# A first close whose output projection is made in three fp32r products of high and low parts

## The reference

```python
Q, K, V = (circulant(layernorm(x), c, b) for c, b in (wq, wk, wv))   # 16 heads of 16
weights = softmax(einsum('bqhd,bkhd->bhqk', Q, K) * scale)
out_merge = einsum('bhqk,bkhd->bqhd', weights, V).reshape(bs, seq_len, dm)
out = circulant(out_merge, wo_c, wo_b)        # the output projection
x = x + out                                   # x1
x = x + moe(layernorm(x))                     # its router needs layernorm(x1) @ gate_W.T
```

## Time and profile before

| | before |
|---|---|
| median of 3 runs | 2192.7 us (2192.51 to 2196.58) |
| the profiled execution's own time | 2198.27 us |
| its span, first to last instruction | 2196.5 us |
| mean granted TensorE clock | 0.947 |
| PE busy over the span | 1971.4 us (90%) |
| ACT busy | 1384.5 us (63%) |
| DVE busy | 1200.6 us (55%) |
| POOL busy | 757.1 us (34%) |
| exponentials of the first attention, L1236 and L1248 | 256 and 256 |
| output projection, L798 | 240 records |

### The profile page before, as it was taken

The page is one execution under the profiler, slowest core; times in us unless marked ns, Lnnn a source line. Parts: engine busy times, 40 slices in busy tenths (PEclk is TensorE's granted clock), DMA queues, the critical chain, the costliest instruction groups (busy, mean ns, idle before and its releaser), DMA issues. The chain is left out here.

```text
span 2196.5 us, 37925 instructions
## 1 busy us (share of the span) xinstructions
PE 1971.4 (90%) x12275; PEld 1136.5 (52%) x12275; DVE 1200.6 (55%) x2196; ACT 1384.5 (63%) x1581; POOL 757.1 (34%) x643
## 2 busy tenths in 40 slices
PE   6999999999946699999999999958789989998797
PEld 5722333333332588888888888846422222222255
DVE  4520242434357624333333333356599999999867
ACT  5589999999933233233233323236589999999833
POOL 2000000100010242344244244111178888888722
PEclk9999999999965699999999999979899999999998
DMA  6744433543110520221221222049725345263021
GB/s 202 229 95 68 81 77 47 116 58 82 35 40 8 232 83 25 90 80 34 86 80 38 82 87 80 23 184 336 213 46 121 58 90 103 42 142 58 2 87 67
DMA packets 76839, 203.64 MB, mean 93 GB/s; under 512 B 13028, under 2 KB 28134, under 8 KB 74536
## 3 DMA queue, kind: packets, MB, share of 16 engines
q1 hardware_dynamic: 66920, 179.22, 30.7%
q0 software_dynamic: 6816, 18.62, 2.5%
q10 hardware_dynamic: 2896, 3.16, 0.6%
HBM read 338.84 MB, written 60.03 MB: 182 GB/s over the span
## 5 line engine op out<-in xcount | busy, mean ns | idle before, releaser
L1202 PE MATMUL psum<-A_qa,A_ka 50*128 50x512 f32 x2048 | 416.4, 472 | 50.3 <-DVE A1f_probs L1280 22.8
L1202 PEld LDWEIGHTS psum<-A_qa,A_ka 50*128 50x128 f32 x2048 | 178.5, 187 | 503.1 <-DVE A1f_probs L1280 266.3
L2350 PE MATMUL psum<-e_w_high,e_xT 128*128 x1136 | 386.9, 402 | 3.9 <-DVE e_xT L2300 3.8
L1386 POOL TENSOR_TENSOR A1f_probs<-A1f_probs,A1f_bias 128x512 f32<-128x512 f32 x256 | 330.2, 1300 | 116.3 <-ACT A1f_probs L1248 116.2
L1236 ACT ACTIVATE A0f_probs<-psum 128x1024 f32<-128x1024 f32 x256 | 307.6, 1201 | 22.7 <-PE psum L1202 21.5
L1280 DVE SCALAR_TENSOR_TENSOR A1f_probs<-psum,A1f_bias 128x1024 f32<-128x1024 f32 x256 | 311.0, 1215 | 15.8 <-PE psum L1202 13.0
L2307 DVE TENSOR_TENSOR e_hT<-psum,e_hT 128x1024 fp32r<-128x1024 f32 x71 | 87.0, 1225 | 422.4 <-ACT e_hT L2271 422.4
L1248 ACT ACTIVATE A0f_probs<-psum 128x1024 f32<-128x1024 f32 x256 | 308.9, 1207 | 0.4 <-PE psum L1202 0.4
L1240 ACT ACTIVATE A1f_probs<-A1f_probs 128x1024 f32<-128x1024 f32 x256 | 272.8, 1065 | 30.3 <-DVE A1f_probs L1280 29.7
L1218 PE MATMUL psum<-A1f_probs,v 128*32 128x512 f32 x2048 | 276.4, 611 | 15.6 <-POOL A1f_probs L1386 13.8
L1218 PE MATMUL psum<-A0f_probs,v 128*32 128x512 f32 x2048 | 274.3, 608 | 0.0
(11 more groups left out here) (280 smaller groups left out, 2708.2 us busy)
## 6 DMA issues: line engine op xcount, KB each, us to landing
e_w_raw<-in_experts SPq DMA_DIRECT2D x73, 3072.0 KB, 10.8
qk_parts<-L_part SPq DMA_DIRECT2D x64, 512.0 KB, 3.7
A_qa<-qk_parts SPq DMA_DIRECT2D x192, 128.0 KB, 4.2
A_ka<-qk_parts SPq DMA_DIRECT2D x192, 128.0 KB, 6.3
om<-results SPq DMA_DIRECT2D x16, 512.0 KB, 8.5
A1f_bias<-tables SPq DMA_DIRECT2D x16, 384.0 KB, 8.5
A1f_bias<-tables SPq DMA_DIRECT2D x16, 320.0 KB, 10.0
L_x<-in_x SPq DMA_DIRECT2D x8, 512.0 KB, 7.5
```

The costliest lines, as they stand in the source:

```text
L1202: mm = e.matmul(ps[:, side * HALF:(side + 1) * HALF], self.qk.ka[rows, s, pair, kt * P:(kt + 1) * P].bitcast(FP32R), self.qk.qa[rows, s, p ...
L1386: e.tensor_tensor(fourth, fourth, self.bias_of(*w[1:], slice(self.FOURTH, GH)).rearrange("p h q -> p (h q)"), ALU.mult).then_inc(self.mult ...
L2350: mm = e.matmul(out, left[part].bitcast(FP32R), moving.bitcast(FP32R), start=start and i == 0, stop=stop and i == 2)
```

## The change

`heavy(u)` now yields 4 tiles of 256 columns for every unit. A tile is six matmuls on fp32r operands: for each of two 128-row chunks, high part of om with high part of wo, high with low, and low with high. POOL makes the parts by two instructions each, a copy that rounds to fp32r and a subtraction, in new jobs `part` that stand right behind the turn of each odd g (16 jobs on 128 x 512 elements), and once for wo at the start. PE's first tile of a unit waits for `parted` in the place of `turned`. Tiles are put into the list in steps kt = 1 and kt = 6 of a half, and in steps kt = 5, 6 and 7 (two in kt = 7) of the very last half. DVE's add is one of 128 x 256 in the place of two of 128 x 128.

```diff
-    def pieces(self, u):
-
-        return ((0, D),) if u == self.LAST else ((0, D // 2), (D // 2, D))
+        self.om_high, self.om_low = (sb(f"c_om_{name}", [P, 2, DC, HALF]) for name in ("high", "low"))
+
+
+
+    def parts(self, b):
+
+        return [("part", 2 * b + half, c) for c in range(DC) for half in range(2)]
 
     def heavy(self, u):
         for t in range(self.T):
-            for a, z in self.pieces(u):
-                yield [("wo", u, t, a, z)] + ([("stats", u, t)] if z == D else [])
+            yield [("wo", u, t), ("stats", u, t)]
...
+        self.part(e, self.wo_high[:, :, :], self.wo_low[:, :, :], self.wo[:, :, :])
+
+    def part(self, e, high, low, whole):
+        steps = self.m.pool
+        a = steps.of(e.tensor_copy(high.bitcast(FP32R), whole))
+        e.wait_ge(steps.sem, a)
+        e.tensor_tensor(low.bitcast(FP32R), whole, high, ALU.subtract).then_inc(self.parted, 1)
 
     def pool(self, e, job):
         kind, u = job[0], job[1]
         s, steps = u % 2, self.m.pool
+        if kind == "part":
+            c, b, half = job[2], u // 2, u % 2
+            e.wait_ge(self.turned, 4 * b + half + 2 * c + 1)
+            if u >= 2:
+                e.wait_ge(self.wo_full, self.wo_count(u - 2, self.T - 1))
+            self.part(e, self.om_high[:, s, c, :], self.om_low[:, s, c, :],
+                      self.omT[:, b, c, half * HALF:(half + 1) * HALF])
         if kind == "fetch":
             e.wait_ge(self.x_in[s], DMA * (u // 2 + 1))
             e.tensor_tensor(self.x[:, s, :, :], self.x[:, s, :, :], repeat(self.bo[:, :], self.T),
...
-            t, a, z = job[2:]
-            b, half = u // 2, u % 2
-            if t == 0 and a == 0:
-                if u == 0:
-                    self.wait_weights(e)
-                e.wait_ge(self.turned, 4 * b + half + 3)
-            at = (half * self.T + t) * P
-            for k in range(DC):
-                mm = e.matmul(ps[:, 0:z - a], self.omT[:, b, k, at:at + P], self.wo[:, k, a:z], start=(k == 0),
-                              stop=(k == DC - 1))
+            t = job[2]
+            if t == 0:
+                e.wait_ge(self.parted, 1 + 4 * (u // 2) + u % 2 + 3)
+            tile = slice(t * P, (t + 1) * P)
+            products = [(om, w, k) for k in range(DC)
+                        for om, w in ((self.om_high, self.wo_high), (self.om_high, self.wo_low), (self.om_low, self.wo_high))]
+            for i, (om, w, k) in enumerate(products):
+                mm = e.matmul(ps[:, 0:D], om[:, u % 2, k, tile].bitcast(FP32R), w[:, k, :].bitcast(FP32R),
+                              start=(i == 0), stop=(i == len(products) - 1))
             mm.then_inc(self.wo_full, 1)
         elif kind == "xn":
             t = job[2]
...
-            e.wait_ge(self.wo_full, self.wo_count(u, t, z))
-            e.tensor_tensor(self.x1[:, s, t, a:z], self.m.wide(slots.slot(job))[:, 0:z - a], self.x[:, s, t, a:z],
+            e.wait_ge(self.wo_full, self.wo_count(u, t))
+            e.tensor_tensor(self.x1[:, s, t, :], self.m.wide(slots.slot(job))[:, 0:D], self.x[:, s, t, :],
                             ALU.add).then_inc(self.wo_out, 1)
...
-                if self.order[at][0] == NG - 1:
-                    u = 2 * self.order[at][1] + half
+                g, b = self.order[at]
+                u = 2 * b + half
+                if g % 2:
+                    work.append(("part", u, g // 2))
+                if g == NG - 1:
                     heavy.extend(close.heavy(u))
                     waiting.append(u)
 
         def begin():
             work.extend(heavy.pop(0))
-            if waiting and len(heavy) % len(list(close.heavy(0))) == 0:
+            if waiting and len(heavy) % close.T == 0:
                 u = waiting.pop(0)
                 light.extend(chain(close.behind(u), close.logits(u)))
 
@@ -1004,9 +1022,9 @@
                     if len(behind) >= self.lag:
                         products()
                     ends = at == last and half == 1
-                    if heavy and (kt in (3, 5, 7) or ends):
+                    if heavy and (kt >= 5 if ends else kt in (1, 6)):
                         begin()
-                        if ends and heavy and kt >= BT - 2:
+                        if ends and heavy and kt == BT - 1:
                             begin()
                     if light:
                         work.extend(light.pop(0))
@@ -1581,8 +1599,9 @@
```

More of the change, by code:

```diff
@@ L674, in __init__ @@
         self.turned, self.wo_full, self.wo_out = sem("c_turned"), sem("c_wo_full"), sem("c_wo_out")
+        self.parted = sem("c_parted")
         self.measured, self.rooted, self.normed = sem("c_measured"), sem("c_rooted"), sem("c_normed")
@@ L684, in allocate @@
         self.wo, self.bo = sb("wo", [P, DC, D]), sb("bo", [P, D])
+        self.wo_high, self.wo_low = sb("wo_high", [P, DC, D]), sb("wo_low", [P, DC, D])
         self.gate, self.gate_rows = sb("gate", [P, DC, EXPERTS]), sb("gate_rows", [P, EXPERTS, D])
@@ L722, in logits, with wo_count @@
             yield [("scale", u)]
-    def wo_count(self, u, t, z):
-        return 2 * self.T * u + (t + 1 if u == self.LAST else 2 * t + (2 if z == D else 1))
+    def wo_count(self, u, t):
+        return self.T * u + t + 1
     def load_weights(self, e):
@@ L748, in sync @@
             if u >= 2:
-                e.wait_ge(self.wo_out, self.wo_count(u - 2, self.T - 1, D))
+                e.wait_ge(self.wo_out, self.wo_count(u - 2, self.T - 1))
             e.dma_start(self.x[:, s, :, :], self.x_src[u, :, :, :]).then_inc(self.x_in[s], DMA)
         elif kind == "store_x1":
-            e.wait_ge(self.wo_out, self.wo_count(u, self.T - 1, D))
+            e.wait_ge(self.wo_out, self.wo_count(u, self.T - 1))
             if u:
@@ L831, in dve @@
             t = job[2]
-            e.wait_ge(self.wo_out, self.wo_count(u, t, D))
+            e.wait_ge(self.wo_out, self.wo_count(u, t))
             n = steps.of(e.bn_stats(self.stats[:, t, :], self.x1[:, s, t, :]))
@@ L1583, in __init__ @@
         self.close = close
-        parts = chain([[("fetch", 0), ("fetch", 1)]], *(chain(close.heavy(u), close.behind(u), close.logits(u))
-                                                        for u in range(close.UNITS)))
+        parts = chain([[("fetch", 0), ("fetch", 1)]],
+                      *(chain([close.parts(u // 2)] if u % 2 == 0 else [], close.heavy(u), close.behind(u),
+                              close.logits(u)) for u in range(close.UNITS)))
         self.jobs = [j for part in parts for j in part]
```

## The result

| | before | after |
|---|---|---|
| median of 7 runs each | 2194.42 us (2192.51 to 2201.33) | 2205.66 us (2199.34 to 2208.83) |
| the profiled execution's own time | 2198.27 us | 2205.16 us |
| its span | 2196.5 us | 2203.1 us |
| mean granted TensorE clock | 0.947 | 0.944 |

The change makes the kernel slower: the ratio is 1.0048, with an interval of 1.0036 to 1.0060, so +10.5 us (+7.9 to +13.2). The profiled executions show +6.9 of it.

The account below looks back on a forecast made before the run. ACT's exponentials were taken to set the pace. Three times eight halves +8.8, the last half -5.0 and the tail +1.5 gave +5.3 us on the median of 2192.7, so 2198.0 us, range 2191 to 2205.

Parts of the forecast that it names:

- main case: The whole kernel gets slower, to 2198.0 us, with its own range of 2194.5 to 2201.5; chance 0.45.
- B: Rival: PE's clock stays low for long behind each stall, a stalled tile costs 8.0 us; +11.3, 2204.0 us; chance 0.15.
- C: Rival: matmul work isn't shortened, 0.96 us per tile, 0.49 lost by each of 21; +9.3, 2202.0 us; chance 0.07.
- three times eight halves: From the turn of u = 0 to that of u = 6: each eight halves cost 8.5 us instead of 5.6, +8.8 in all.
- the last half: Tiles of u = 6 move to kt = 5, 6, 7, 7; the stall and its low clock go: -5.0 us.
- the tail: Behind the turn of u = 7, PE starts 2.1 us later because parts come between: +1.5 us.
- stalled first tile: At u = 0, 2, 4 PE waits for turn and part: 4.7 us at full clock, 1.5 for the clock, 6.2 each.
- ordinary tile: Each of 21 tiles in the eight halves outside the stalls costs 0.33 us, bounds 0 and 0.49.
- ring: A tile shifts the ring of three, so scores wait for an exponential one place later: 0.28 to 0.35 us lost.
- 12 other parts: POOL's part jobs outside the stalls and the tail run beside work that does not wait: no cost.
- A: Rival: PE's clock is back within 1 us, a stalled tile costs 5.2 us; +1.2, 2193.9 us; chance 0.25.
- D: Rival: the spacing decides, the 21 ordinary tiles cost nothing and the clock holds; -8.0, 2184.7 us; chance 0.08.

Follow-up runs that it names:

- kept_busy: The changed kernel with 14 small matmuls on constants ahead of PE's wait for the first tile of u = 0, 2 and 4; 2201.81 us, ratio 1.0043.
- late_4_7: The changed kernel with its tiles in steps kt = 4 and 7 in the place of 1 and 6; 2184.68 us, ratio 0.9962.
- even_steps: The changed kernel with tiles in steps kt = 0 and 4, the last part job in two and POOL's bias add in four; 2182.54 us, ratio 0.995.
- parts_beside: The kernel before with the 16 part jobs added on POOL, their results read by nobody; 2193.2 us, ratio 0.9992.
- bias_in_four: The changed kernel with POOL's bias add made in four instructions of 128 x 256; 2207.89 us in a single execution.
- split_last: The changed kernel with the last part job (u = 7) made in two, 128 and 384 columns; 2205.96 us in a single execution.
- plain_1_6: The changed kernel's tiles and steps, but each tile in two fp32 matmuls straight from omT, without parts on POOL; 2196.12 us, ratio 1.001.
- late_3_6: The changed kernel with its tiles in steps kt = 3 and 6 in the place of 1 and 6; 2180.91 us in a single execution.

## Why the prediction was right on the sign and short on the size

On the base that the prediction used, 2192.7 us, the ratio gives 2203.2: slower, as forecast, but by 10.5 us and not 5.3. That lies inside the stated 2191 to 2205 and outside the main case's own 2194.5 to 2201.5: the mechanism was right, but the range held only because it had been widened for rivals B and C. The sum by its own steps, against the stage of the profiled execution:

| term | predicted | measured |
|---|---|---|
| three times eight halves | +8.8 | +12.4 |
| the last half | -5.0 | -4.6 |
| the tail | +1.5 | +1.3 to the last statistics, +0.7 to the sinkhorn |
| sum | +5.3 | +8.5 in the stage |

*The stalled first tile* was right in place and nearly so in size. PE idle was to be some 4.5 us, released by POOL's subtraction: 4.44. ACT idle some 5 us: 5.63. The clock near 0.5: 0.50. The full-clock loss of 4.7: 4.6, by kept_busy. The clock's 1.5, from an assumed 3.7 us at the lower level: 1.85 on average, for 5.4, 4.6 and 3.4 us at it. Together 6.4 instead of 6.2, 0.6 us over three of them; the three groups of eight halves, less 21 ordinary tiles and two collisions, give 6.4 each too.

*The ordinary tile* was mis-sized: 0.33 predicted, 0.43 measured in late_4_7, 21 x 0.10 = 2.0 us of the 3.6 that are missing in the eight halves. The prediction took six starts of 0.12 us, 0.72 in all, from a run of equal matmuls. The timeline of the kernel after shows the edges of such a tile among scores and products:

```profile
243.12 0.38 PE L813 MATMUL psum<-wo_high,c_om_high 128*128 128x256 f32 x1
...
243.34 0.28 PE L813 MATMUL psum<-wo_low,c_om_high 128*128 128x256 f32 x1
...
243.81 0.28 PE L813 MATMUL psum<-wo_high,c_om_low 128*128 128x256 f32 x1
...
244.01 0.74 PE L1220 MATMUL psum<-A_qa,A_ka 50*128 50x512 f32 x4
```

The first matmul needs 0.22 us to the next start and the last one 0.20, the four between 0.12: 0.89 (0.90 to 0.92 for most tiles). The step exceeds ACT's by 1.66 + 0.89 - 1.83 = 0.72, less the slack of 0.3, some 0.42. So with the right length the formula meets the 0.43; its 0.72 us for a tile was the mis-sized term. The slack itself depends on the steps: at kt = 0 and 4 the same tile cost (120.02 - 117.33) / 8 = 0.34 (even_steps).

*The collision* with the bias add was not foreseen: the prediction gave DVE's adds "nothing" and weighed a contact of POOL with DVE in the tail only. Two of them cost 1.06 us. With 2.0 and 0.6 this closes the 3.6. The bias add isn't new; what is new is a tile in kt = 1, directly behind the turn whose divide it holds up, in a ring with 0.3 us of slack.

*The last half* came out at 16.13 for 15.7: its two tiles in kt = 7 lie on PE alone and take 0.89 each instead of 0.72, which is 0.34 of the 0.43. The stall and the low clock of u = 6 are gone, as forecast.

*The tail*: PE waited 4.53 us for the part, the last statistics end 10.33 us behind the last turn instead of 9.00, +1.3 for the predicted 1.5. But to the sinkhorn it is +0.7 only, since the clock behind the statistics was 0.84 in this execution and 0.74 in that of the kernel before; kernels with the same tail took 20.0 to 22.3 us for it. That the tail came out below its forecast is chance, and it hides a part of the three terms that were too small. The rows with the part beside them:

```profile
620.59 2.65 DVE L857 TENSOR_SCALAR c_xn<-c_x,c_mv,c_root 128x256 f32<-128x256 f32 x4
...
622.91 0.36 PE L813 MATMUL psum<-wo_high,c_om_high 128*128 128x256 f32 x1 [4.53 <-POOL c_om_low L774]
...
624.23 0.42 DVE L843 TENSOR_TENSOR c_x<-psum,c_x 128x256 f32<-128x256 f32 x1 [0.99 <-PE psum L813]
```

DVE's four rows operations took 2.65 us where they took 1.34, the full 1.3 us of the prediction's upper bound, but DVE was then idle 0.99 us for PE, so they cost nothing here. The rule that the prediction named (the Trainium skill, SBUF — State Buffer, section "Who interferes with whom") agrees with this row and, for an operation with two SBUF inputs against POOL, with the divide of 1.70 us.

*The 12 other parts* at nothing: right, parts_beside shows no cost and eight halves of 122.92.

The rivals: A fell, as it allowed the clock 0.5 us per stall and the clock cost 1.4 to 2.2. D fell with the ordinary tile of 0.43; late_4_7 came to its 2184.7 by another way, by having no stall, and that the numbers meet is chance. B's time of 2204.0 is close to what was measured, and by its mechanism it is wrong all the same: it wanted 3.3 us of clock per stall, and the longest seen was 2.6. C's tile of 0.96 was nearer than the forecast's 0.72, and its cause, a tile longer than six starts of 0.12 us, is that of the largest missing term.

The stage of the profiled execution explains 8.5 us of the 10.5 (7.9 to 13.2) of the runs. In bias_in_four and split_last, whose edits should not slow it, the stage was +10.4 and +10.1 against the kernel before: in the first mostly because the tail took 22.0 us, in the second because the halves with a stall took up to 22.56, both with more time at the lower clock. So the profiled execution of the kernel after seems to be one of the shorter ones, and the rest needs nothing from the later stages; two further executions don't prove it. What stays open is why the clock stays low for 3.4 us once and for 6.6 us another time behind the same wait, and why it differs in the tail.

## What to carry to other kernels

Put work that waits for another engine's result so many steps behind it that the result is there; in a list that several engines walk, a helper engine's 2 us of preparation cost nothing measurable three steps later, and 2 us and a longer fall of the clock directly behind its source. Before a faster form of an operation is judged by its length, count how often it enters the ring: fewer, wider tiles, with the steps that go with them, gave 1.6 of the 2.2 us per eight halves here. Take the spacing of a matmul from records with the same neighbours, since the two edges of the group of six took 0.42 of its 0.89 us.

## What the runs showed of the hardware

- The same 2.42 us of idle PE in one kernel left the granted clock at 1.00 once and took it to 0.50 twice (plain_1_6). An idle time of 4.44 us took it to 0.50 in nine of nine places, for 3.4 to 6.6 us (after, bias_in_four, split_last). Idle times of 0.78 us (late_3_6) and 1.02 us (kept_busy) left it at 1.00, three places each. The price of the low clock was 1.2 to 2.6 us each time and grew with the time at it.
- Six fp32r matmuls over 256 columns take 0.89 to 0.92 us among matmuls of other forms, not 6 x 0.12; the two fp32 matmuls that give the same tile take 1.06. So the three-product form saves some 0.15 us of PE per tile and costs POOL 0.9 us for it (two parts of 1.9 us for four tiles).
- A DVE divide of 128 x 256 with two SBUF inputs took 1.70 us beside a POOL add of 2.39 us (2.33 at most, in kept_busy), and 0.42 alone. It ended 0.28 us behind the POOL instruction, and with the add in four the longest was 0.96.
